# The last round of a token sort placed by 0/1 products in PSUM, and what that moves

## The reference, cut to what matters

```python
xn = _layernorm(x)
s = x1 + corrected @ W_le + b_le             # x1: xn filtered by FFT, corrected: its 24 bits mended
logits = xn @ router_w.T;  probs = softmax(logits)
topk_vals, topk_idx = top_k(probs, 2)
topk_w = topk_vals / (topk_vals.sum(-1) + 1e-6)
expert_out = einsum('nh,eho->eno', xn, expert_weights)      # 8 experts, 512 x 512 each
out = ((expert_out[topk_idx] + probs[topk_idx]) * topk_w).sum(0)
return x + s * silu(out)
```

## Time and profile before

| what | us |
|---|---|
| median of three runs | 1247.49 (1242.68 to 1249.14) |
| the profiled execution, whole | 1248.74 |
| its span | 1246.9 |
| PE busy | 1122.4 (90%) |
| DVE busy | 1089.1 (87%) |
| POOL busy | 877.0 (70%) |
| ACT busy | 509.0 (41%) |

### The profile page before, as it was taken

The page is one execution under the profiler, slowest core; times in us unless marked ns, Lnnn a source line. Parts: engine busy times, 40 slices in busy tenths (PEclk is TensorE's granted clock), DMA queues, the critical chain, the costliest instruction groups (busy, mean ns, idle before and its releaser), DMA issues. The chain is left out here.

```text
span 1246.9 us, 26774 instructions
## 1 busy us (share of the span) xinstructions
PE 1122.4 (90%) x6265; PEld 608.3 (49%) x6266; DVE 1089.1 (87%) x2625; ACT 509.0 (41%) x1151; POOL 877.0 (70%) x873
## 2 busy tenths in 40 slices
PE   5998889700799999999999999999999999999996
PEld 4554555400355455555555554555555555555553
DVE  6799979992888689989999998999999899999985
ACT  4576556560577333323333333333333333333332
POOL 1126654765888378778888887888888788888874
PEclk8999889955799999999999999999999999999999
DMA  8659999300465576666666666666666666666664
GB/s 320 238 192 200 195 168 214 64 18 24 129 185 184 143 167 174 173 168 177 172 171 176 176 173 170 169 172 177 174 174 172 167 178 172 178 170 173 177 168 108
DMA packets 217433, 208.75 MB, mean 167 GB/s; under 512 B 166783, under 2 KB 166783, under 8 KB 213298
## 3 DMA queue, kind: packets, MB, share of 16 engines
q1 hardware_dynamic: 184370, 124.31, 42.2%
q0 software_dynamic: 31872, 79.79, 21.6%
q10 hardware_dynamic: 1152, 4.19, 1.4%
HBM read 123.36 MB, written 47.12 MB: 137 GB/s over the span
## 5 line engine op out<-in xcount | busy, mean ns | idle before, releaser
L1366 PE MATMUL banks<-w_hi,arena 128*128 (+1 forms) x1136 | 431.6, 380 | 9.5 <-DMA arena<-arena 5.0
L1367 PE MATMUL banks<-w_lo,arena 128*128 (+1 forms) x1136 | 431.3, 380 | 0.0
L1368 PE MATMUL banks<-w_hi,arena 128*128 (+1 forms) x1136 | 431.1, 379 | 0.0
L700 ACT ACTIVATE arena<-xbuf,inf 128x512 f16<-128x512 f32 x156 | 112.6, 722 | 509.6 <-DVE xbuf L1168 509.6
L516 POOL DMA_INDIRECT inf<-token_info,gidx x156 | 194.7, 1248 | 54.1 <-issue 54.1
L514 POOL DMA_INDIRECT xbuf<-in_L_attn_x,gidx x156 | 176.3, 1130 | 77.4 <-issue 67.0
L493 POOL DMA_INDIRECT pair_tokens<-tok,slot x128 | 133.8, 1045 | 122.7 <-DVE slot L1038 81.0
L554 POOL TENSOR_TENSOR xbuf<-xbuf 128x512 f32<-128x512 f32 x128 | 162.7, 1271 | 40.1 <-DVE xbuf L1237 35.9
L1366 PEld LDWEIGHTS banks<-w_hi,arena 128*128 128x128 f16 x1136 | 111.2, 98 | 136.7 <-issue 15.0
L1368 PEld LDWEIGHTS banks<-w_hi,arena 128*128 128x128 f16 x1136 | 111.4, 98 | 131.5 <-issue 0.8
L520 POOL DMA_INDIRECT out<-xbuf,sidx x128 | 140.4, 1097 | 40.7 <-issue 40.4
(11 more groups left out here) (284 smaller groups left out, 1713.5 us busy)
## 6 DMA issues: line engine op xcount, KB each, us to landing
xbuf<-in_L_attn_x SPq DMA_DIRECT2D x32, 1024.0 KB, 13.7
arena<-extra_sums SPq DMA_DIRECT2D x128, 256.0 KB, 2.7
arena<-in_L_ffn_expert_weights SPq DMA_DIRECT2D x8, 1024.0 KB, 11.7
extra_sums<-arena SPq DMA_DIRECT2D x28, 256.0 KB, 2.1
token_info<-info ACTq DMA_DIRECT2D x8, 512.0 KB, 12.8
xbuf<-in_L_attn_x,gidx POOLq DMA_INDIRECT x156, 3.6
inf<-token_info,gidx POOLq DMA_INDIRECT x156, 2.8
pair_tokens<-tok,slot POOLq DMA_INDIRECT x128
```

Source lines behind the costliest of these rows:

```text
L700: nc.scalar.activation(hi4[ring(i, k)], uv2[:, b], ACT.Copy, scale=inf2[:, k, 1:2]).then_inc(hi_ready, 1)
L1366: mm(ps, hi[:, c], wh, start=(c == 0), stop=False)
L1367: mm(ps, hi[:, c], wl, start=False, stop=False)
L1368: end = mm(ps, lo[:, c], wh, start=False, stop=(c == C - 1))
```

## The change

- POOL scatters only the first seven rounds' tokens (`range(R - 1)`), and waits for these.
- The eighth round's slots are no longer written as indices. DVE takes the totals from bank 7 and computes each token's place in the sorted list directly (`place_f`), splits it in tile and position (`place_tile`, `place_lane`), and makes for each of 16 columns two 128x128 arrays in 16 bits: `in_tile` (1 where the column's token lies in the tile) and `in_lane` (the token's number, where it lies at the position). PE sums the 16 products in bank 0; the result (`tokTl`) enters `tile_tok` by a third product beside the two of the rows read back. The rows are masked by `settled`, the end of a pair without its tokens of the eighth round.
- Token numbers are counted from the start of the eighth round (`FIRST_TOKEN`), so that these are small; the cast to `tile_tok` adds the offset.
- The norm product on PE and its root on ACT move from behind the eighth round into step 3 of the seventh (`NORM_ROOT_AT`), where PE waits for the root; `scales` moves to step 1 of the eighth.
- `place` of the eighth round goes; `weigh` follows `choose` at once, and the table's operations are interleaved with those of the places.
- Behind `tile_tok` now stand: the diagonals, `tslot`, the live flags, `low_sums(0)` and two low parts. The others follow between the first tiles (2, 3) and behind extra steps 1, 2, 3 and 9 (`LOW_AT`). The marks of the main tiles follow behind steps 14 and 18. The waits of ACT, SP, POOL and PE are adapted to this.
- The differences of the experts lie in another order in the arena (`DIFF_AT`), and the tiles' parts at other addresses.

```diff
     EXPERT_ORDER = (*range(1, NE), 0)
...
-    EARLY = NE - 3
+    DIFF_AT = (6, 1, 3, 4, 5, 0, 2, 7)
+    LOW_AT = {1: 4, 2: 5, 3: 6, 9: 7}
+    FIRST_TOKEN = (R - 1) * P * TB - 1
...
+        in_tile, in_lane = (arena[:, 16 * E + i * TB * P // 2:16 * E + (i + 1) * TB * P // 2].bitcast(F16).rearrange(
+            "p (t n) -> p t n", t=TB) for i in range(2))
...
+        NORM_ROOT_AT = (R - 2, U - 1)
...
-            for i in range(R):
+            for i in range(R - 1):
                 scatter(i, i % 2)
 
             for b in range(2):
-                pool.wait_ge(scattered[b], 16 * T // 2)
+                pool.wait_ge(scattered[b], 16 * TB * (R // 2 - b))
...
+                if (i, k) == NORM_ROOT_AT:
+                    act.wait_ge(norm_red, 1)
+                    nc.scalar.activation(norm_all[:, :], psum[:, 2, 0:NE], ACT.Sqrt, scale=float(E)).then_inc(norm_root, 1)
...
-            act.wait_ge(norm_red, 1)
-            nc.scalar.activation(norm_all[:, :], psum[:, 2, 0:NE], ACT.Sqrt, scale=float(E)).then_inc(norm_root, 1)
...
-            act.wait_ge(tiles_ready, 3)
+            act.wait_ge(tiles_ready, 1)
...
+                if (i, k) == (R - 1, 1):
+                    scales()
...
-            place(R - 1, 1, R // 2 - 1)
             weigh(R - 1)
-            scales()
-
-
-            count, end, start, tile_of, base, within, before, live, again = (tq[:, c] for c in range(9))
-            dve.wait_ge(slot_ready, R)
+
+
+            count, end, start, tile_of, base, within, before, live, again, seen, newest, settled = (tq[:, c] for c in range(12))
+            place_f, place_tile, place_lane = (last_at[:, c] for c in range(3))
+            totals = psum[:, 7, 0:NQ * TB].rearrange("p (q t) -> p q t", q=NQ)
+            earlier = psum[:, 6, 0:NQ * TB].rearrange("p (q t) -> p q t", q=NQ)
             V.memset(tvals[:, 0, 0], 1.0)
             V.memset(tcmp[:, NQ:NQ + 1], 0.0)
-            V.memset(before, 0.0)
-            V.memset(again[:, 0:1], 0.0)
-            link(V.tensor_tensor(count, used[:, :], region_c, ALU.subtract))
+            V.tensor_tensor(seen, used[:, :], region_c, ALU.subtract)
+            V.tensor_scalar(tokf[:, :], tokf[:, :], float(P * TB), None, ALU.add)
+            dve.wait_ge(rank_mm, R)
+            link(V.tensor_reduce(newest, totals, AXX, ALU.add))
+            link(V.tensor_tensor(count, seen, newest, ALU.add))
             link(V.tensor_tensor_scan(end, tvals[:, 0, 0], count, 0.0, ALU.mult, ALU.add))
+            V.tensor_tensor(settled, end, newest, ALU.subtract)
             link(V.tensor_tensor(start, end, count, ALU.subtract))
             V.tensor_scalar(tcmp[:, 0:NQ], start, base_c, None, ALU.is_le)
+            V.tensor_tensor(seen, seen, start, ALU.add)
             link(V.tensor_scalar(tile_of, start, 1.0 / P, -(P - 1) / (2.0 * P), ALU.mult, ALU.add))
+            V.tensor_tensor(totals[:, :, 0], totals[:, :, 0], seen, ALU.add)
             V.tensor_tensor(tone[:, :], tcmp[:, 0:NQ], tcmp[:, 1:NQ + 1], ALU.subtract)
             link(V.tensor_scalar(tile_of, tile_of, 12582912.0, None, ALU.add))
+            V.tensor_tensor_scan(ranks.rearrange("p q t -> p (q t)"), carry_c, psum[:, 7, 0:NQ * TB], 0.0, ALU.mult, ALU.add)
             V.tensor_tensor(tvals[:, 0, 0], region_c, start, ALU.subtract)
             link(V.tensor_scalar(tile_of, tile_of, 12582912.0, None, ALU.subtract))
-            V.tensor_copy(tvals[:, 0, 1], end)
+            V.tensor_tensor(slots[:, :, :], earlier, ranks[:, :, :], ALU.add)
+            V.tensor_copy(tvals[:, 0, 1], settled)
             link(V.tensor_scalar(base, tile_of, float(P), None, ALU.mult))
...
-            V.tensor_tensor(tvals[:, 1, 2], end, base, ALU.subtract)
+            V.tensor_tensor(tvals[:, 1, 2], settled, base, ALU.subtract)
             link(V.tensor_tensor(within, start, base, ALU.subtract))
             V.tensor_tensor(tvals[:, 1, 0], region_c, within, ALU.subtract)
             V.tensor_copy(tvals[:, 1, 1], within)
...
             link(V.tensor_reduce(tsel[:, :, :], tvals[:, :, :, :], AXX, ALU.add))
-            V.tensor_tensor(trow[:, 0:1], tsel[:, 0, 0:1], base_c, ALU.add)
-            V.tensor_copy(trow[:, 1:2], tsel[:, 1, 0:1]).then_inc(rows_ready, 1)
-
+            V.tensor_copy(trow[:, 1:2], tsel[:, 1, 0:1])
+            V.tensor_tensor(trow[:, 0:1], tsel[:, 0, 0:1], base_c, ALU.add).then_inc(rows_ready, 1)
+
+
+            link(V.tensor_tensor(slots[:, :, :], slots[:, :, :], pairs[:, :, :], ALU.mult))
+            V.tensor_copy(to_tile[:, 0, NX:NT], ident[:, :])
+            link(V.tensor_reduce(place_f, over(slots), AXX, ALU.add))
+            V.tensor_scalar(to_tile[:, 0, 0:NX], tile_of, lane_c, None, ALU.is_equal)
+            link(V.tensor_scalar(place_tile, place_f, 1.0 / P, -(P - 1) / (2.0 * P), ALU.mult, ALU.add))
+            V.tensor_scalar(to_tile[:, 1, 0:NX], tile_of, tsel[:, 1, 3:4], None, ALU.is_equal)
+            link(V.tensor_scalar(place_tile, place_tile, 12582912.0, None, ALU.add))
+            V.tensor_scalar(to_tile[:, 1, NX:NT], iota_c, tsel[:, 1, 3:4], None, ALU.is_equal)
+            link(V.tensor_scalar(place_tile, place_tile, 12582912.0, None, ALU.subtract))
+            V.tensor_tensor(tend[:, :], tsel[:, 0, 1:2], base_c, ALU.subtract)
+            link(V.scalar_tensor_tensor(place_lane, place_tile, -float(P), place_f, ALU.mult, ALU.add))
+            for t in range(TB):
+                V.tensor_scalar(in_tile[:, t], iota_h[:, :], place_tile[:, t:t + 1], None, ALU.is_equal)
+                V.tensor_scalar(in_lane[:, t], iota_h[:, :], place_lane[:, t:t + 1], tokf[:, t:t + 1], ALU.is_equal,
+                                ALU.mult).then_inc(last_marks, 1)
+            dve.wait_ge(last_mm, 1)
+            V.tensor_copy(tokTl, psum[:, 0, 0:P])
+
+
+            dve.wait_ge(rows_loaded, 32)
+            link(V.tensor_copy(tokTf[:, :, :], tokT[:, :, :]))
+            V.scalar_tensor_tensor(tokTf[:, 0], iota_c, tend[:, 0:1], tokTf[:, 0], ALU.is_lt, ALU.mult)
+            link(V.scalar_tensor_tensor(tokTf[:, 1], iota_c, tsel[:, 1, 2:3], tokTf[:, 1], ALU.is_lt, ALU.mult))
+            V.scalar_tensor_tensor(tokTf[:, 1], iota_c, tsel[:, 1, 1:2], tokTf[:, 1], ALU.is_ge, ALU.mult).then_inc(rows_float, 1)
+            dve.wait_ge(toks_mm, 1)
+            V.tensor_scalar(tile_tok[:, :], psum[:, 5, 0:NT], float(FIRST_TOKEN), None, ALU.add).then_inc(tiles_ready, 1)
+
+
+            V.memset(before, 0.0)
+            V.memset(again[:, 0:1], 0.0)
+            V.tensor_scalar(tdiag[:, 0], ident[:, :], tsel[:, 0, 2:3], None, ALU.mult)
+            V.tensor_scalar(tdiag[:, 1], ident[:, :], tsel[:, 0, 3:4], None, ALU.mult)
+            link(V.tensor_tensor(count, to_tile[:, 0, 0:NX], iota_c[:, 0:NX], ALU.mult))
+            V.tensor_reduce(tslot[:, :], count, AXX, ALU.max).then_inc(diag_ready, 1)
             low = 0
             high = NE - 1
             for head in range(NE - 1, 1, -1):
-                V.tensor_copy(before[:, high:high + head - 1], end[:, low:low + head - 1])
+                last = V.tensor_copy(before[:, high:high + head - 1], end[:, low:low + head - 1])
...
-            for c in range(EARLY):
+            for c in range(2):
                 low_parts(c)
             V.memset(acc2[:, 1], 0.0).then_inc(acc_init, 1)
-            dve.wait_ge(exps_mm, 1)
...
-            V.tensor_copy(tile_tok[:, :], psum[:, 5, 0:NT]).then_inc(tiles_ready, 1)
+
+            def marks_alike():
+
+                dve.wait_ge(exps_mm, 1)
+                V.tensor_copy(tile_exp[:, :, :], psum[0:1, 2, 0:3 * P].rearrange("o (v t) -> o v t", v=3)).then_inc(tiles_ready, 1)
+                dve.wait_ge(spread_mm, 1)
+                V.tensor_tensor(onehot, psum[:, 3, 0:2 * P].rearrange("p (s t) -> p t s", s=2).unsqueeze(3).broadcast_to([P, T, 2, NE]),
+                                iota_c[:, 0:NE].unsqueeze(1).unsqueeze(1).broadcast_to([P, T, 2, NE]),
+                                ALU.is_equal).then_inc(marks_ready, 1)
+
+            def marks_scaled():
+
+                dve.wait_ge(marks_ready, 1)
+                V.tensor_tensor(onehot, onehot, unscale[:, :].unsqueeze(1).unsqueeze(1).broadcast_to([P, T, 2, NE]),
+                                ALU.mult).then_inc(marks_ready, 1)
...
-            dve.wait_ge(tiles_ready, 3)
             V.memset(parts[0][:, 2 * E + 96:2 * E + P], 0.0)
             V.memset(parts[1][:, 2 * E + 96:2 * E + P], 0.0).then_inc(pad_ready, 1)
             for k in range(3):
                 halves_of(0, k)
                 low_part(0, k)
-                low_parts(EARLY + k)
+                if k:
+                    low_parts(k + 1)
             halves_of(0, 3)
             for n in range(NX):
                 extra_step(n)
+                if n in LOW_AT:
+                    low_parts(LOW_AT[n])
+                if n == NX // 2:
+                    marks_alike()
+                if n == NX // 2 + 4:
+                    marks_scaled()
...
                     turn(*nxt, 2)
```

(30 more changed lines are left out.)

53 lines of the change are left out of this document (18 added, 35 removed).

## The result

On the first chip the kernel before took 1247.84 us (median of 4), the changed one 1235.32 (4 runs, 1231.95 to 1237.14): ratio 0.9897 (95%: 0.9861 to 0.9933), 12.5 us less where 24.5 were forecast, and just outside the forecast's 1217 to 1234. Repeated on two other chips the ratio was 0.9931 (0.9910 to 0.9952) and 0.9933 (0.9907 to 0.9958). Chips differ (the kernel before took 1238 to 1318 us on them), so ratios are compared, and stretches between events of one trace.

What follows compares the result with a forecast made beforehand. GpSimd's queue of scatters was taken to bound the start of the extra steps. First extra product 28.0 us earlier, less 3.5 lost in the steps, gives 24.5: 1224.2 profiled, 1223 as median; range for 8 in 10 1217 to 1234.

Steps and rivals of the forecast that it cites:

- norm wait: Seventh round: TensorE waits for ScalarE's root behind the norm product, between 0.57 and 1.8 us, taken as 0.9.
- Rows known: Eighth round on VectorE: rows to read known at 261.8, before GpSimd can use them at 264.3, so hidden.
- Scatters over: GpSimd's last scatter, of the seventh round, ends at 261.3: 260.42 plus 0.9 of delay from the norms.
- Read-back: GpSimd starts reading the rows 3.0 us after the last scatter's end; rows loaded at 268.8.
- The marks: VectorE's 32 new 128x128 marks before the token table: 0.13 us each, between 0.06 and 0.25, together 4.2 us.
- The queue's hole: GpSimd's 5.14 us hole at its 114th transfer might recur in the read-back: nothing to 4.8 us, taken as 1.7.
- third product waited for: Token table: two products are waited for 1.50 us, the third adds 0.75.
- rival B: Around the read-back, VectorE's short instructions lock GpSimd out: 7.9 us later than forecast, 1231 us; chance 0.18.
- part 4: VectorE's work moved behind the token table and into the extra steps: 13.4 us against 14 us idle; 3.5 us lost.
- three low halves in a row: Low parts of 2.4 us behind extra steps 1, 2 and 3: TensorE waits 1.6 and 1.9 us, 3.5 lost.
- rival C: Extra steps: gathers slowed by low parts land late, three steps, 6.6 us at most, 1229 us; chance 0.10.
- rival E: Extra steps: TensorE's clock stays at 1.2 GHz, up to 6.07 us a step, 1259 us; chance 0.05.

Runs made afterwards that it cites:

- both additions out: Changed kernel with marks ahead of the first tile and without late low halves of experts 5, 6, 7 and 0: ratio 0.9939 to the kernel before, stretch 83.0 us.
- added wait: Changed kernel plus VectorE waiting in each extra step for GpSimd's coefficient of the tile before: 1224.11 us against 1238.47, ratio 0.9907.
- marks ahead: Changed kernel with both operations on the main tiles' marks moved from behind steps 14 and 18 to ahead of the first tile: ratio 0.9916, stretch 87.5 us.
- the kernel with an input from PSUM: Changed kernel with eight late low-half operations reading one input from PSUM instead of two from SBUF: ratio 0.9881 to the kernel before, stretch 93.7 us.
- the changed kernel's second trace: The changed kernel once more, unaltered, on another chip where the kernel before takes 1317 us: ratio 0.9931, stretch 95.4 us.

## Why the prediction was wrong

**What held.** The chain was read rightly: with the scatters gone the table comes early, at 271.9 to 272.2 instead of 304.39. Term by term: norm wait 0.7 us (0.9 forecast). Rows known at 258.6, ahead of their use. Scatters over at 258.8 (261.3: the round was 1.7 us earlier, and the norms' delay did not reach them). Read-back 3.8 us behind the last scatter (3.0). The marks are dearer: 32 in 6.2 us, 0.19 each, not 0.13; that is the length of the dearer neighbour which the prediction named and went below. The queue's hole cost nothing (1.7). The third product waited for: 2.02 us in all (2.25). VectorE comes 8.8 us behind the table (8.8). With the 3.9 us that the seventh round was earlier, the first extra product stands at 295.7 for 294.7. That it comes so near is in part luck: the marks were 2.0 us dearer, and the hole priced at 1.7 did not come.

**The queue's hole.** Neither as a count (no hole at the 113th and 114th indirect DMA) nor as rival B: the reads are issued at 262.56 and 263.96, in the midst of the marks, at 0.97 and 0.96 us. The Trainium skill, SBUF — State Buffer (section "Who interferes with whom"), says that `tensor_scalar` can enter a mode that locks GpSimd out; beside these marks, which are such instructions, no read-back was held up, so no run here shows that. What made the hole of 5.14 us stays open. The main loop's holes of 1.9 us come every 35 tiles as before.

**The step that failed** is part 4's "The single ones fit, since VectorE works three steps ahead". Its first half, the three low halves in a row, was right: 3.5 us forecast, 3.9 measured in the first trace (1.8 of them before step 5 and as much before step 6). The other 9.2 us lie in later steps, where the prediction set 13.4 us of work against 14 us of VectorE's idle time. It counted one engine. Work added to VectorE holds GpSimd up as well, and GpSimd was the one with no time: 0.2 to 0.3 us in a step of 3.04. It was in the profile: 66.5 us busy and some 14 of issuing gaps in 80. With both additions out the steps lose 0.2 us besides ScalarE's pauses, so the loss is theirs whole. Where no gather was held (the low half behind step 9 with an input from PSUM), the single one did fit: 0.2 us lost. The prediction even says so under rival C, but priced it for three steps and as a passing matter. Rival C's kind was right, its place wrong (1229 at most): the hold-ups of steps 1 to 9 are repaid in steps 10 and on, with the marks on top.

How it runs, by the experiments: an operation of VectorE with two inputs from SBUF stops a gather beside it (1.5 to 2.7 us instead of 1.0 beside low halves, 4.25 beside the second mark operation); the gathers come late; VectorE is then behind, also by the first mark operation, which itself holds nothing; it works two or three tiles through without a pause, and a GpSimd instruction is held for most or all of it (3.3, 5.7, 7.1 and 7.5 us seen); VectorE runs out of tiles and idles. The added wait breaks the third link and wins 4.4 to 7.0 us of stretch. The 9.0 us that it leaves in the steps are in part VectorE's own load: 3.1 us behind the three low halves stay even when no gather is held, and 1.2 behind the second mark operation with no gather held. How the rest divides isn't shown. Whether it is one port that both engines want, the runs don't show directly; that PSUM in place of one SBUF input frees the gathers speaks for it. The Trainium skill, SBUF — State Buffer (section "Who interferes with whom"), has the rule: a VectorE instruction with two inputs in SBUF contends with a GpSimd instruction that reads SBUF, one with at most one, outside the two-port modes, does not. The traces agree (1.5 to 2.1 us beside two, 1.0 beside one, in the rows above), with one addition: GpSimd's hold-up does not end with the instruction, but reaches over 16 that begin after it (7.11 us) and 18 (7.52 us).

**Not settled**: the hand-over's 2.1 us. It is 18.0 before and 16.9 there with the added wait, 18.2 with both additions out, 18.9 to 19.4 with the added wait, 20.0 to 20.4 in the changed kernel, and in the other kernels without the wait 20.0 to 22.0 (22.0 with the marks ahead). It is long where GpSimd is late, but doesn't go with the loss in the steps; the changed kernel's last accumulation also waited 4.13 us for a store.

## What to carry to other kernels

Idle time of the engine that gets the work is half the account: list, for each engine it shares memory or buffers with, how much that one has to spare in a step, and what holds it up. Where two engines feed each other in a ring and one has 0.3 us to spare in 3, a single delay was not made good here within 16 steps, and one lump of work turned into small losses in later steps. A wait that makes the faster engine pause once a step can be worth more than the time it takes; test it on the undisturbed kernel as well, where it must do nothing. And split a stretch into its steps before two traces are compared: two of 83.0 and 83.1 us were alike by luck here.

## What the runs showed of the hardware

- GpSimd's one-column product, 0.19 us when alone, took 7.1 and 7.5 us while VectorE worked gaplessly; an indirect gather up to 5.74 us instead of 1.0. Beside the first mark operation (2.27 us, one input in PSUM) a gather took 1.02 us.
- A 128x1024 operation of VectorE took 1.28 us with two inputs from SBUF and 1.22 with one from PSUM; the gathers beside it 1.5 to 2.1 us and 1.0.
- A 128x128 mark from 16-bit data starts 0.16 us after the one before if that has one operation, and 0.22 if it has two; those from 32 bits of the earlier trace rows are 0.29 long.
- TensorE was back at full clock 3.2 us after its first extra product (at 295.0, 291.82 and on), 3.5 us before the change, and 2.8 to 5.4 us in the other traces, with which the first step varied from 4.0 to 5.1 us. Waits of 1 to 2.4 us in the changed kernel's steps did not lower the clock (0.98 over the stretch), so rival E had no ground. Of two waits of 2.9 and 3.0 us one (the kernel with an input from PSUM, at 406.3) came with 3.4 us at 0.5, the other (the changed kernel's second trace, at 431.8) with none.
- ScalarE paused for 1.5 to 3.0 us with its input ready in four of the seventeen traces, all from two of the chips.
